# Mixture-of-experts results: weighted on chip and added into two sums per token by indirect DMA, in place of one stored row per choice

## What is computed

```
x = x + 0.5 * ffn(layernorm(x))
x = x + attn(layernorm(x))
x = x + 0.5 * ffn(layernorm(x))
```

```
a = silu(x @ Wg[e]) * (x @ Wu[e]) * w[token, e]
y += a @ Wd[e]            # and 0.05 * the same with cWg, cWu, cWd of chunk e // 2
```

## Time and profile before

| what | value |
|---|---|
| median of 3 runs | 670.13 us (669.44 to 670.83) |
| profiled execution, span from first to last instruction | 683.6 us |
| PE busy in it | 554.9 us, 81% |
| DVE, ACT, POOL busy | 351.7, 157.6 and 322.9 us |
| moved by DMA | 70.00 MB |

### The profile page before, as it was taken

One profiled execution on the slowest core, in us unless ns is written; L12 is line 12 of the kernel. 1 busy time (PEld: TensorE's weight loads), 2 busy tenths in 40 slices (PEclk: granted clock), 3 DMA queues, 4 the chain that ended last, 5 costly groups with the idle time before them and its releaser, 6 DMA issues. The chain is left out here.

```text
span 683.6 us, 10495 instructions
## 1 busy us (share of the span) xinstructions
PE 554.9 (81%) x3134; PEld 473.8 (69%) x3134; DVE 351.7 (51%) x1123; ACT 157.6 (23%) x422; POOL 322.9 (47%) x348
## 2 busy tenths in 40 slices
PE   5149999998805999999999999995269999999820
PEld 5028888887603888888888888884158888888710
DVE  6933334433348656664765666568733443343325
ACT  3001222222224322312222231223002222222211
POOL 0364666666335444433533443420746666666331
PEclk9999999999956999999999999998559999999965
DMA  7969622223172010111111011108322222223153
GB/s 247 315 199 293 199 89 86 90 84 95 44 284 87 24 32 32 47 49 36 41 48 32 31 33 46 39 1 308 124 54 84 87 86 88 87 90 94 58 202 132
DMA packets 33880, 70.00 MB, mean 102 GB/s; under 512 B 6288, under 2 KB 15888, under 8 KB 33808
## 3 DMA queue, kind: packets, MB, share of 16 engines
q1 hardware_dynamic: 22672, 42.88, 19.2%
q0 software_dynamic: 8832, 24.13, 11.6%
q10 hardware_dynamic: 2304, 2.10, 0.9%
HBM read 53.88 MB, written 15.20 MB: 101 GB/s over the span
## 5 line engine op out<-in xcount | busy, mean ns | idle before, releaser
L826 DVE COPY oT_all<-bank 128x256 f32<-128x256 f32 x92 | 39.1, 425 | 176.1 <-PE bank L1009 164.6
L430 POOL DMA_INDIRECT decay_all<-xn_dram,ids x92 | 89.1, 968 | 79.7 <-PE bank L1009 71.1
L439 POOL DMA_INDIRECT z_dram<-probs_all,dest x92 | 90.7, 986 | 49.0 <-issue 24.6
L490 POOL TENSOR_TENSOR kqT<-rope 128x512 f32<-128x512 f32 x36 | 45.9, 1274 | 130.1 <-DVE rope L883 130.1
L1022 PE MATMUL bank<-w_ch_sb,oT_all 128*128 x368 | 98.0, 390 | 0.0
L1019 PE MATMUL bank<-w_exp_sb,oT_all 128*128 x368 | 82.1, 347 | 9.1 <-issue 2.5
L1019 PEld LDWEIGHTS bank<-w_exp_sb,oT_all 128*128 128x128 f32 x368 | 63.2, 195 | 29.0 <-issue 26.4
L600 ACT ACTIVATE rot<-bank 128x224 f32<-128x224 f32 x92 | 32.9, 357 | 201.8 <-PE bank L1022 199.0
L1022 PEld LDWEIGHTS bank<-w_ch_sb,oT_all 128*128 128x128 f32 x368 | 69.8, 196 | 5.3
L1112 PE MATMUL bank<-split_sb 128*128 128x512 f32 x240 | 65.2, 407 | 1.8 <-ACT split_sb L565 0.9
L902 DVE TENSOR_TENSOR split_sb<-bank,split_sb 128x512 fp32r<-128x512 f32 x32 | 22.1, 692 | 66.2 <-ACT split_sb L651 66.2
(11 more groups left out here) (133 smaller groups left out, 960.2 us busy)
## 6 DMA issues: line engine op xcount, KB each, us to landing
w_exp_sb<-w_exp SPq DMA_DIRECT2D x32, 384.0 KB, 10.1
w_ch_sb<-w_ch SPq DMA_DIRECT2D x16, 384.0 KB, 10.3
decay_all<-decay SPq DMA_DIRECT2D x16, 256.0 KB, 2.6
w_down_sb<-w_down SPq DMA_DIRECT2D x16, 192.0 KB, 11.3
kqT<-z_dram SPq DMA_DIRECT2D x6, 512.0 KB, 6.8
rope<-z_dram SPq DMA_DIRECT2D x6, 512.0 KB, 5.1
xn_dram<-xn_sb ACTq DMA_DIRECT2D x16, 128.0 KB, 6.7
wq_all<-wq SPq DMA_DIRECT2D x16, 128.0 KB, 2.2
```

Source lines behind the costliest of these rows:

```text
L430: pool.indirect_dma_start(out=xg[s], out_offset=None, in_=xn_dram[l][:, :], in_offset=bass.IndirectOffsetOnAxis(ap=ids[:, t:t + 1], axis=0 ...
L439: pool.indirect_dma_start(out=z_dram[l][:, :], out_offset=bass.IndirectOffsetOnAxis(ap=dest[:, t:t + 1], axis=0), in_=y_sb[s], in_offset=N ...
L490: nc.gpsimd.tensor_tensor(dst, rope_a[r % 2], rope_b[r % 2], ALU.add).then_inc(roped, 1)
L826: nc.vector.tensor_copy(xgT[s], xT_ps[s][:, 0:D].rearrange("p (k t) -> p k t", k=KD)).then_inc(xgT_ready[s], 1)
```

## The change

Each row of `xn_dram` becomes 264 floats: 256 of the token, then its four weights (times 0.5) and the same four times 0.05. ScalarE stores the weights there with one transfer, in pieces of 32 bytes, once VectorE has computed them; the computation of `wgt` moves ahead of `tile_ge` in the routing. The gathered row therefore brings its token's weights. VectorE picks the one weight of the slot with a product against a one-hot (`slot_part`) and a sum (`slot_wgt`), and multiplies it into the activations in `product`. So the result rows are already weighted, and POOL's scatter adds them into a sum in DRAM. There are two sums per layer, `acc_dram[l][0]` and `[1]`; slot tiles alternate between them, and a scatter waits for the one before it on the same sum. Sum 0 starts as x itself (copied from the input for layer 0, stored from `x_sb` for layer 1), sum 1 starts as zero. Combining is then two loads and one addition a token tile.

```diff
             for c in range(NCH - BEHIND):
                 load_chunk(c)
+                if c == 2:
+                    sp.dma_start(acc_dram[0][0][0:T, :], x_in[:, :]).then_inc(acc_filled[0], 16)
+                    sp.wait_ge(zero_ready, 1)
+                    clear(0, 0, TT)
+                    clear(0, 1, 0)
...
             pool.wait_ge(xn_stored[l], 16 * TT)
+            pool.wait_ge(wgt_stored[l], 16)
             pool.wait_ge(ids_ready, l + 1)
...
                 pool.wait_ge(xg_used[s], n)
+                if l * SLOT_TILES + t >= XG:
+                    u, m = slot_of(l, t - XG)
+                    pool.wait_ge(xgT_ready[u], m + 1)
...
                 pool.wait_ge(y_copied, l * SLOT_TILES + t + 1)
-                pool.indirect_dma_start(out=z_dram[l][:, :],
+                if t >= ACCS:
+                    pool.wait_ge(acc_added[l][t % ACCS], t // ACCS * 16)
+                pool.indirect_dma_start(out=acc_dram[l][t % ACCS][:, :],
                                         out_offset=bass.IndirectOffsetOnAxis(ap=dest[:, t:t + 1], axis=0),
-                                        in_=y_sb[s], in_offset=None).then_inc(y_scattered[l][t % YB], 16)
+                                        in_=y_sb[s], in_offset=None, compute_op=ALU.add).then_inc(acc_added[l][t % ACCS], 16)
...
+            act_e.wait_ge(wgt_ready, l + 1)
+            act_e.dma_start(xn_dram[l][:, D:ROW].rearrange("(t p) k -> p t k", p=P),
+                            wgt[:].rearrange("p t a k -> p t (a k)")).then_inc(wgt_stored[l], 16)
...
+                nc.vector.tensor_tensor(slot_part[:, s, :, :], xg[g][:, D:ROW].rearrange("p (a k) -> p a k", a=2),
+                                        slot_hot[:, t, :].unsqueeze(1).broadcast_to([P, 2, TOP_K]), ALU.mult).then_inc(slot_part_ready[s], 1)
                 nc.vector.tensor_copy(xgT[s], xT_ps[s][:, 0:D].rearrange("p (k t) -> p k t", k=KD)).then_inc(xgT_ready[s], 1)
+                dve.wait_ge(slot_part_ready[s], n + 1)
+                nc.vector.tensor_reduce(slot_wgt[:, s, :], slot_part[:, s, :, :], AX.X, ALU.add).then_inc(slot_wgt_ready[s], 1)
...
-        def combine(dve, l, i, k):
-
-            n = l * TT + i
-            if k == 0:
-                dve.wait_ge(x_part, n + 1)
-            return nc.vector.scalar_tensor_tensor(x_sb[:, i, :], z_sb[n % ZB][:, k, :], wgt[:, i, k:k + 1], x_sb[:, i, :],
-                                                  ALU.mult, ALU.add)
+        def combine(dve, l, i):
+
+            for a in range(ACCS):
+                dve.wait_ge(acc_in[l * TT + a * TT // 2 + i // 2], 16)
+            nc.vector.tensor_tensor(x_sb[:, i, :], x_sb[:, i, :], sum_sb[:, i, :], ALU.add).then_inc(x_done, 1)
```

The loads of sum 0 are issued by SyncE, those of sum 1 by ScalarE, two token tiles (256 KB) each:

```diff
+        def load_sums(eng, l, a, i):
+
+            dst = x_sb if a == 0 else sum_sb
+            eng.dma_start(dst[:, i:i + 2, :], acc_dram[l][a][i * P:(i + 2) * P, :]
+                          .rearrange("(t p) d -> p t d", p=P)).then_inc(acc_in[l * TT + a * TT // 2 + i // 2], 16)
```

More of the change, by code:

```diff
@@ L221, in macaron_kernel @@
         xg_ready = [sems(f"xg_ready{l}_", XG) for l in range(2)]
-        y_scattered = [sems(f"y_scattered{l}_", YB) for l in range(2)]
+        acc_added = [sems(f"acc_added{l}_", ACCS) for l in range(2)]
         results_stored = sem("results_stored")
@@ L347, in _, with clear @@
             sp.dma_start(key_decay_sb[:], key_decay[:, :]).then_inc(const_in, 16)
+            def clear(l, a, first):
+                tiles = (T + P) // P - first
+                sp.dma_start(acc_dram[l][a][first * P:, :].rearrange("(t p) d -> p t d", p=P),
+                             zero_sb.unsqueeze(1).broadcast_to([P, tiles, D])).then_inc(acc_filled[l], 16)
             def load_chunk(c):
@@ L387, in load_head @@
                 sp.dma_start(wo_sb[u], wo[h, :, :]).then_inc(wo_in[u], 16)
[L389 to L395, removed]
+            clear(1, 0, TT)
+            clear(1, 1, 0)
+            sp.wait_ge(results_stored, 1)
+            for i in range(0, TT, 2):
+                load_sums(sp, 0, 0, i)
+                if i == 0:
+                    load_kv(0)
+            load_head(0)
+            sp.dma_start(cos_sb, cos[:, :]).then_inc(const_in, 16)
+            sp.dma_start(sin_sb, sin[:, :]).then_inc(const_in, 16)
             for h in range(1, H):
@@ L403, in _ @@
                 sp.dma_start(w_exp_sb[:, 2 * c * EXP_COLS:2 * (c + 1) * EXP_COLS], w_exp[c, :, :]).then_inc(w_reloaded, 16)
-            load_results(sp, 1)
+            for i in range(TT):
+                sp.wait_ge(x2_copied, i + 1)
+                sp.dma_start(acc_dram[1][0][i * P:(i + 1) * P, :], x_sb[:, i, :]).then_inc(acc_filled[1], 16)
+            sp.wait_ge(results_stored, 2)
+            for i in range(0, TT, 2):
+                load_sums(sp, 1, 0, i)
             for i in range(TT):
@@ L569, in norm_act @@
             if s == 1:
-                for i in range(3):
-                    scale_results(act_e, 0, i)
+                act_e.wait_ge(results_stored, 1)
+                act_e.wait_ge(acc_filled[1], 32)
+                for i in range(0, TT, 2):
+                    load_sums(act_e, 0, 1, i)
             for i in range(TT):
                 n = s * TT + i
-                if s == 1 and i + 3 < TT:
-                    scale_results(act_e, 0, i + 3)
                 act_e.wait_ge(rvar_ready, n + 1)
@@ L656, in _ @@
             moe_act(act_e, 1, last_residuals)
-            for i in range(TT):
-                scale_results(act_e, 1, i)
+            act_e.wait_ge(results_stored, 2)
+            for i in range(0, TT, 2):
+                load_sums(act_e, 1, 1, i)
         def norm_dve(dve, tick, s, beside=None):
```

123 lines of the change are left out of this document (47 added, 76 removed).

## The result

The changed kernel takes 686.6 us in the median of 4 runs (685.43 to 689.68), the kernel before 670.3 (669.44 to 670.83). The ratio is 1.0254, 95% interval 1.0229 to 1.028: **2.5% slower**. The forecast was 662 us and faster; rival 1, POOL as the bound, is what happened.

A forecast was written before the change was run, and what follows sets the result against it. PE's time plus four stages in which PE waits, two for routing and two for combining, bound the kernel. Terms -10.6 - 10.2 + 2.5 + 1.3 + 4.3 + 4.5 + 0.5 = -7.7 us took 670.1 to 662 us, range 650 to 688.

The forecast's parts named there:

- rival 1: Slot-tile loops: adding scatters make POOL the bound beyond 1.42 us each; 667 at 1.5 times, 705 at twice; chance 0.2.
- The adding scatter: POOL's scatters: land in 4.1 us, issue stays 0.99; hidden in the loops, +2.5 and +1.3 us in the tails.
- long tiles: Slot-tile loops: 17 of 37 profiled intervals take 3.0 to 3.3 us, the others 2.8; 2.99 us a tile.
- Rival 2: Slot-tile loops: the two sums' own chain decides if an addition lands after over 5.7 us; 712 at 7 us; chance 0.1.
- Tails: Each layer's last scatters: the final adding one starts and lands later, +2.5 us in layer 0, +1.3 in layer 1.
- Combining: Loading and adding results after each loop: shorter by 10.6 us in layer 0 and 10.2 in layer 1.
- The start of layer 0: Before the first transposes: fills keep the queue full, delaying the weights' store and first gather; +4.5 us (0 to 8.8).
- Layer 1's term of 0.5: Start of layer 1: its first gather waits for the weights' store to land; +0.5 us (0 to 2.1).
- VectorE's small operations: Slot-tile loops: two added operations delay the up matmul in long tiles by 0.12 us each; +4.3 us (0 to 9).
- The end: Stores of `out` and the program's end behind them: stay as they are, no gain or loss forecast.
- all of 4: Whole kernel: the forecast itself, 652 to 668 us, chance 0.58, counted wholly as faster.
- a third of 1: Share of the case of POOL as the bound (chance 0.2) that was counted as faster.

The follow-up runs named there:

- E3: Kernel before, with only layer 1's scatters made adding, into cleared rows each written once; no sums, no order between scatters: 679.56 us, ratio 1.0149.
- E0: The kernel before, unchanged, run and profiled once more: 668.59 us, span 666.8.
- E4: E2 with scatters over four sums instead of two, only two of them loaded, half the results left out: 676.25 us, ratio 1.0129.
- E1: Changed kernel with plain scatters that overwrite the sums' rows instead of adding, all waits kept: 655.12 us, ratio 0.9783.
- E2: Changed kernel with the fills of layer 0's sums moved from behind the third weight chunk to behind the tenth: 682.7 us, ratio 1.0187.
- E6: Against the kernel before: weights applied on chip, plain scatters, four rows read back, additions shared by POOL and VectorE: 670.62 us, ratio 1.0029.
- E8: E2 with each scatter five gathers behind its own instead of eight: 690.13 us, ratio 1.0309.
- E5: E2 with scatters adding only 128 of 256 columns into half-wide sums never loaded: 670.72 us, ratio 1.0031, with four slot tiles fewer in layer 1.
- E7: E2 with each scatter six gathers behind its own instead of eight: 683.16 us, ratio 1.0206.

## Why the prediction was wrong

**The failed step.** "The adding scatter" bounded only the time from start to landing (3.05 to 5.06, taken as 4.1; measured 3.77 and 3.86) and left POOL's part at the plain 0.99 (measured 1.584), so that in the loop it was "hidden at either end". "POOL needs 2.56 of 2.99 us: hidden" has both numbers wrong: it needs 3.18, of 2.82. E3 shows the first alone, E0 the second. From the numbers now: the adding costs 3.18 - 2.82 = 0.36 us on each tile behind the eighth of a layer, 13.0 us for the 36 of layer 0 and 14.4 for the 40 of layer 1: an estimate for loop and tail without the chain. E4, without the chain's waits, is above E1 in loop and tail by 17.4 and 10.4 us, 13.9 in the mean; that one layer is above the estimate and the other below it isn't explained. Two things that E1 lacks stand in layer 0 of E4: the clearing of two further sums, and 3.9 us in which PE idles ahead of five gate and up matmuls without a releaser that the profile shows. The chain adds 4 to 6 us a layer on top (E4 against E2).

**Rival 1** had the mechanism right, with a threshold of 1.42 us. With 2.82 us tiles it is 1.25. It thought of "a third access to describe", found against it that gather and scatter cost the same, and gave it 0.2. Its price at 1.5 times (667) fell short of the measured 1.6 times (686.6), for it took PE's long tiles as its base and left the tail out. Rival 2, the two sums' chain in the loop, didn't occur: an addition landed in 3.8 us, under the rival's threshold of 5.7.

**Tails.** +2.5 and +1.3 forecast, +8.1 and +5.1 measured. The working looked at the last scatter of each sum alone. With POOL behind PE, eight scatters of 1.55 + 0.30 us are left when the gathers end, and those of one sum stand 4.4 us or more apart. Its plain landing of 3.05 us was one long case; the usual one takes 2.4 to 2.5.

**Combining.** -10.6 and -10.2 forecast, -8.4 and -10.0 measured. Pairs landed as read from the earlier trace rows (first 4.3 us). The projection came 19.8 us behind the load and not 17.4, as the second pair of sum 0 came late (2.63 us of VectorE's wait, above); the bound of 8.8 was just missed. The last addition ends 10.1 us behind the first load of its layer, forecast 9.0.

**The start of layer 0.** +4.5 forecast (0 to 8.8), +6.3 measured, with the mechanism named: the store took 11.2 us in the full queue, where 9.5 was the longest of its kind. The prediction expected PE at 49.4; it began at 51.49. (The fills are 2.36 MB, which at 298 GB/s take 7.9 us and not 7.2.)

**Attention and routing.** Layer 1's term of 0.5 can't be told from the 1.6 us here. That 1.6 also stands in E1, E2, E6 and E8, and not in E4, E5 and E7, and 1.3 of it is PE's clock. In all runs but E3 (the clearing) routing's choice of the four largest logits begins 249.5 us behind the first projection, within 0.1 us. It takes 5.5 to 5.7 us in these five and 4.1 to 4.2 in all others. While it ran, in the changed kernel and in E0 (length, PE, PEld, DVE, ACT, POOL, clock, DMA share, GB/s):

```profile
477.00:482.60 5.60, 4.00 (x20) 3.87 (x20) 4.07 (x25) 2.32 (x4) 0.00 (x0) 0.50 1.04 395
...
459.30:463.50 4.20, 2.43 (x19) 1.99 (x18) 3.86 (x25) 2.44 (x4) 0.00 (x0) 1.00 1.03 386
```

In the five the granted clock fell to 1.2 GHz some 249 us behind the first projection, in the others at 252 or later. Why it falls earlier in some is open. The three executions with the routing of before (before, E0, E3) are all among the fast ones; of the eight with the changed routing five are slow and three fast.

**VectorE's small operations.** +4.3 forecast on the strength of the long tiles. These don't exist in E0, E1, E6 or layer 0 of E3. In E1, where POOL isn't the bound, the loops are 2.4 and 0.3 us longer than in E0, and 2.0 of that is PE's clock in the first tiles. The term should have been 0.7 at most, which its lower bound of 0 allowed for.

**The end.** The prediction let it stay; it fell to 2.6 us from the last addition to the end, from 7.2. The stores of `out` aren't the reason: the last one lands 1.8 to 2.2 us behind the last addition in every run. What comes behind it is POOL's DRAIN, an instruction at its program's end. E0, then the changed kernel (POOLq and SPq are the sequencers, which hand an engine its instructions; duration in ns three times, then the start in us):

```profile
L52 POOLq DRAIN  x1: 10097/10097/10097, 656.4 to 656.4; - x1
...
L52 SPq DRAIN  x1: 7/7/7, 661.6 to 661.6; - x1
...
L54 POOLq DRAIN  x1: 5543/5543/5543, 675.3 to 675.3; - x1
...
L54 SPq DRAIN  x1: 7/7/7, 687.3 to 687.3; - x1
```

In E0 POOL's ends at 666.5, 4.9 us behind SyncE's, and the span ends 0.2 later. Where POOL adds in combining (before, E0, E3, E6) it begins its DRAIN late, and the span ends with it; where it doesn't (the changed kernel and all made from it) the DRAIN is over before the stores have landed, and the span ends 0.4 us behind the last landing. So these 4.6 us belong to the change, as a gain: the prediction put at nothing what taking POOL's additions away does there. What sets a DRAIN's length (4.9 to 10.2 us in these runs) is open. It matters: 4.8 of the 13.8 us by which E1's span lies below E0's are there.

**Chances.** The prediction's chances are off by little: all of 4 and a third of 1 make 0.65 for faster, not 0.63, and 0.29 are left for slower.

## What to carry to other kernels

Price an indirect transfer on two clocks: how long its issuing engine is held, and how long until it lands. An adding one lands 1.4 us later than a plain one, which two sums in turn hide in the loop, and holds POOL 0.6 us longer, and where POOL has 0.26 us of room per step that decides the loop. Before the engine with the least room is given more work, take the room from an ordinary execution: here the one profile at hand overstated it by two thirds. And a queue that is full when a short store is issued delays whoever waits for that store (11.2 us to landing here, 4.6 with the fills moved); fills that are needed late belong behind it.

## What the runs showed of the hardware

- An adding indirect scatter of 128 rows holds POOL 1.584 us in the mean of 92, and 1.55 when only scatters follow each other; the plain one takes 0.987 (E1). It is the same at 512 and 1024 B a row (E5). The time from the end of the issue to landing is 3.77 - 1.55 = 2.2 us; for the plain one it is 2.41 - 0.97 = 1.4 (E1), and was 3.05 - 0.97 = 2.1 in one case.
- An adding scatter makes 144 packets where a plain one makes 48, and three queues agree on it (13440, 17664, and 16896 = 88 x (48 + 144) in E5).
- The Trainium skill, DMA: Bandwidth & Descriptors, "Anatomy of one DMA", calls the generation of descriptors "small, variable" beside some 2 us of fixed time. Behind the issue 2.2 us of the adding form agree with it; the plain form's 1.4 are less. If POOL's time is that generation, the small part doesn't agree: it is 0.99 or 1.58 us, and the 1.58 bound the changed kernel.
- POOL's DRAIN at the end of the program takes 4.9 to 10.2 us, and the span waits for it: 10.1 us in E0, 5.1 of them behind the last landing of a store.
